# Row statistics written straight into lasting tiles, and an earlier combination in the inputs of the last attention

## What is computed

```python
x = L0(x)                              # window attention and an MLP, each behind a row norm
x = x + L1(group_norm(x))              # Fourier mixing
t = t + L2_attn(row_norm(t))           # landmark attention
t = t + L2_ffn(row_norm(t))            # two of eight experts for each token
t = t + L3_attn(row_norm(t))           # full attention, 12 heads of 16
t = t + L3_ffn(row_norm(t))            # one of eight experts for each token

def row_norm(v, eps):
    return (v - mean(v, -1)) / sqrt(var(v, -1) + eps)
```

## Time and profile before

| | |
|---|---|
| median of three runs | 1279.95 us (1279.7 to 1282.09) |
| the profiled execution | 1278.96 us, of it the span 1277.1 us |
| busy, share of the span | PE 82%, PEld 62%, DVE 46%, ACT 34%, POOL 22% |
| instructions | 21213; POOL 473 of those counted as busy |
| stage `l3p` and its last stores | about 902 to 987 us of the span |

### The profile page before, as it was taken

The page is one execution under the profiler, slowest core; times in us unless marked ns, Lnnn a source line. Parts: engine busy times, 40 slices in busy tenths (PEclk is TensorE's granted clock), DMA queues, the critical chain, the costliest instruction groups (busy, mean ns, idle before and its releaser), DMA issues. The chain is left out here.

```text
span 1277.1 us, 21213 instructions
## 1 busy us (share of the span) xinstructions
PE 1045.2 (82%) x7522; PEld 794.2 (62%) x7523; DVE 591.8 (46%) x1420; ACT 435.0 (34%) x880; POOL 286.9 (22%) x473
## 2 busy tenths in 40 slices
PE   6795999996998887999898379999376898767890
PEld 5594878874656665787897336666255455465670
DVE  4742655543114555455655634444364677331112
ACT  3653255553323222344440011111054466412330
POOL 5454301102001111000013042220563212103104
PEclk9865999998999998899787589999698999958895
DMA  7444843300112000100003621120244432044534
GB/s 89 120 115 126 188 92 86 93 7 1 38 62 72 16 0 0 50 2 1 1 2 100 180 56 50 49 49 31 59 107 102 129 97 72 3 142 113 148 112 105
DMA packets 118625, 91.41 MB, mean 72 GB/s; under 512 B 33010, under 2 KB 110924, under 8 KB 117900
## 3 DMA queue, kind: packets, MB, share of 16 engines
q1 hardware_dynamic: 106935, 76.31, 23.1%
q0 software_dynamic: 4992, 10.23, 3.7%
q10 hardware_dynamic: 6613, 3.74, 1.1%
HBM read 64.38 MB, written 28.12 MB: 72 GB/s over the span
## 5 line engine op out<-in xcount | busy, mean ns | idle before, releaser
L1227 DVE TENSOR_REDUCE l0a_nmax<-l0a_psS 98x2 f32<-98x392 f32 x96 | 54.2, 566 | 54.1 <-PE l0a_psS L1042 50.1
L871 DVE TENSOR_REDUCE l3a_nmax<-l3a_psS 128x2 f32<-128x512 f32 x96 | 62.0, 686 | 33.7 <-PE l3a_psS L725 33.4
L2428 POOL DMA_INDIRECT l2e_X<-xn,token_at x40 | 38.4, 961 | 128.2 <-PE l2e_psX L2443 74.9
L2493 ACT ACTIVATE l2e_H<-l2e_psH 128x512 f32<-128x512 f32 x40 | 21.7, 595 | 131.2 <-PE l2e_psH L2455 131.2
L827 ACT ACTIVATE l3a_PT<-l3a_psST 128x512 f32<-128x512 f32 x96 | 54.7, 596 | 29.0 <-PE l3a_psST L755 28.4
L2473 PEld LDWEIGHTS l2e_psY<-W2T,l2e_HT 128*128 128x128 f32 x320 | 51.4, 190 | 18.3 <-issue 18.2
L1177 ACT ACTIVATE l0a_PT<-l0a_psST 98x392 f32<-98x392 f32 x96 | 47.2, 497 | 42.2 <-PE l0a_psST L1084 41.9
L2473 PE MATMUL l2e_psY<-W2T,l2e_HT 128*128 x320 | 57.3, 332 | 3.4 <-DVE l2e_HT L2514 2.1
L2452 PE MATMUL l2e_psH<-W1T,l2e_XT 128*128 x80 | 40.9, 635 | 2.8 <-issue 2.0
L2520 DVE COPY l2e_Y<-l2e_psY 128x384 f32<-128x384 f32 x20 | 11.1, 557 | 65.1 <-PE l2e_psY L2473 65.1
L725 PE MATMUL l3a_psS<-l3a_KS,l3a_QS 96*128 96x256 bf16 x192 | 37.3, 275 | 3.9 <-DMA l3a_KS<-kd 2.9
(11 more groups left out here) (534 smaller groups left out, 2752.6 us busy)
## 6 DMA issues: line engine op xcount, KB each, us to landing
l3a_QS<-qd SPq DMA_DIRECT2D x72, 64.0 KB, 2.2
l3a_KS<-kd SPq DMA_DIRECT2D x72, 64.0 KB, 2.2
expert_W<-in_L_ffn_w SPq DMA_DIRECT2D x8, 576.0 KB, 4.7
rd<-l0q_r_p SPq DMA_DIRECT2D x24, 168.0 KB
ys<-l2e_Y SPq DMA_DIRECT2D x20, 192.0 KB, 1.9
l0a_QS<-qd SPq DMA_DIRECT2D x54, 64.0 KB
l0a_KS<-kd SPq DMA_DIRECT2D x54, 64.0 KB
W2T<-in_w2t SPq DMA_DIRECT2D x2, 1536.0 KB
```

Of the source, the lines that this page charges most:

```text
L871: nc.vector.tensor_reduce(nmax[k % 2][:, TI * u:TI * (u + 1), s], psS[item % 2][:, :].rearrange("p (t k) -> p t k", t=TI), AX.X, ALU.max, ...
L1227: mx = nc.vector.tensor_reduce(nmax[k % 2][0:WQ, 2 * j:2 * (j + 1), s], psS[item % 2][0:WQ, 0:2 * W0].rearrange("p (t k) -> p t k", t=2), ...
L2428: pool.indirect_dma_start(out=X[p % RING][:, t, :], out_offset=None, in_=G["xn"], in_offset=bass.IndirectOffsetOnAxis(ap=G["token_at"][:, ...
```

## The change

There are now two classes. `LoopStats` is the old one, used in the Fourier stage alone. The new `LnStats` has no tiles `mv` and `rstd`: `bn_aggr` writes mean and variance into a lasting tile `MV` (one pair per row tile), the add reads the variance there, and the power writes `RSTD` itself and raises `kept`. Its waits are plain ones. `MEAN` is now a view of `MV`, every second element. In `combined_inputs`, VectorE's `combine(i + 2)` stands ahead of the two remainders of image i.

```diff
--- before.py
+++ after.py
@@ -136,6 +136,40 @@
     def __init__(self, st, G, eps):
         self.nc, self.G, self.eps = st.nc, G, eps
         self.part = st.sb("stat_part", [P, 2, TI, 6])
+        self.ve = st.sb("stat_ve", [P, 2, TI])
+        self.exponent = st.sb("stat_exponent", [P, TI])
+        self.parts_done, self.mv_done, self.pow_done, self.kept = st.sems("stat_parts stat_mv stat_pow stat_kept")
+
+    def init(self, pool):
+
+        pool.sem_inc(self.kept, 2)
+        self.nc.gpsimd.memset(self.exponent[:, :], -0.5).then_inc(self.pow_done, 1)
+
+    def vector(self, nc, dve, i, u, *ready):
+
+        for sem, value in ready:
+            dve.wait_ge(sem, value)
+        dve.wait_ge(self.kept, i + 1)
+        for t in range(TI):
+            nc.vector.bn_stats(self.part[:, u, t, :], self.G["X"][:, TI * i + t, :]).then_inc(self.parts_done, 1)
+        dve.wait_ge(self.parts_done, TI * (i + 1))
+        for t in range(TI):
+            nc.vector.bn_aggr(self.G["MV"][:, TI * i + t, :], self.part[:, u, t, :]).then_inc(self.mv_done, 1)
+
+    def gpsimd(self, nc, pool, i, u):
+        pool.wait_ge(self.mv_done, TI * (i + 1))
+        nc.gpsimd.tensor_scalar(self.ve[:, u, :], self.G["MV"][:, TI * i:TI * (i + 1), 1], self.eps, None, ALU.add).then_inc(self.pow_done, 1)
+        pool.wait_ge(self.pow_done, i + 2)
+        nc.gpsimd.tensor_tensor(self.G["RSTD"][:, TI * i:TI * (i + 1)], self.ve[:, u, :], self.exponent[:, :], ALU.pow).then_inc(self.kept, 1)
+
+
+class LoopStats:
+
+
+
+    def __init__(self, st, G, eps):
+        self.nc, self.G, self.eps = st.nc, G, eps
+        self.part = st.sb("stat_part", [P, 2, TI, 6])
         self.mv = st.sb("stat_mv", [P, 2, TI, 2])
         self.ve = st.sb("stat_ve", [P, 2, TI])
         self.rstd = st.sb("stat_rstd", [P, 2, TI])
@@ -162,7 +196,7 @@
         pool.wait_ge(self.pow_done, 2 * i + 2)
         nc.gpsimd.tensor_tensor(self.rstd[:, u, :], self.ve[:, u, :], self.exponent[:, :], ALU.pow).then_inc(self.pow_done, 1)
         wait_all(pool, self.G["steady"], (self.pow_done, 2 * i + 3))
-        nc.gpsimd.tensor_copy(self.G["MEAN"][:, bass.ds(TI * i, TI)], self.mv[:, u, :, 0])
+        nc.gpsimd.tensor_copy(self.G["MV"][:, bass.ds(TI * i, TI), 0], self.mv[:, u, :, 0])
         nc.gpsimd.tensor_copy(self.G["RSTD"][:, bass.ds(TI * i, TI)], self.rstd[:, u, :]).then_inc(self.kept, 1)
 
 
@@ -1431,7 +1465,7 @@
         XC, SQ, XN, XS = two("XC", [P, TI, C]), two("SQ", [P, TI, C]), two("XN", [P, TI, C]), two("XS", [P, TI, C])
         FX, Z1, C1 = two("FX", [CH, 2, 3 * NF]), two("Z1", [CH, 2, 2 * NF]), two("C1", [CH, 2, 2 * NF])
         Z2, C2 = two("Z2", [SR, 2, 2, 2, CH]), two("C2", [SR, 2, 2, 2, CH])
-        stats = LnStats(st, G, 1e-5)
+        stats = LoopStats(st, G, 1e-5)
         psA = [st.ps(f"psA{u}") for u in range(2)]
         psB = [[st.ps(f"psB{u}{a}") for a in range(2)] for u in range(2)]
         w_in, zeroed, mean_mm, mean_done, xc_done, sq_done, var_mm, var_done, eps_done, std_done, rstd_done, xn_done, xs_done = st.sems(
@@ -2822,10 +2856,10 @@
                 u = i % 2
                 if i + 1 < B:
                     norm(i + 1)
+                if i + 2 < B:
+                    combine(i + 2)
                 qp.vector(nc, dve, QF[u][:, :, :], i, u)
                 kp.vector(nc, dve, KF[u][:, :, :], i, u)
-                if i + 2 < B:
-                    combine(i + 2)
                 qp.third(nc, dve, i, u)
                 kp.third(nc, dve, i, u)
             dve.wait_ge(pads_done, 2)
@@ -2930,9 +2964,10 @@
     def __init__(self, nc, w, consts, ctx):
         self.nc, self.w, self.consts, self.ctx = nc, w, consts, ctx
         self.G = {"consts": consts, "steady": ctx.enter_context(nc.semaphore("steady"))}
-        self.sb(ctx, X=(P, NT, C), MEAN=(P, NT), RSTD=(P, NT), ident=(P, P), early0=(P, EARLY), early1=(P, EARLY))
+        self.sb(ctx, X=(P, NT, C), MV=(P, NT, 2), RSTD=(P, NT), ident=(P, P), early0=(P, EARLY), early1=(P, EARLY))
         for name, n, dt in (("tri", P, BF16), ("onesb", P, BF16), ("earlier", NT * E + E, BF16), ("count", P, I32), ("token", NT, F16)):
             self.G[name] = ctx.enter_context(nc.sbuf_tensor(name, [P, n], dt))
+        self.G["MEAN"] = self.G["MV"][:, :, 0]
         self.dram(xw=(B * T, C), xr=(B * T, C), band=(NH, P * TW), xn=(B * T, C))
         self.dram(BF16, qd=(B, 3 * C * T), kd=(B, 3 * C * T))
```

## The result

The changed kernel takes 1263.9 us (median of 4 runs, 1260.85 to 1267.32) against 1279.83 for the kernel before on the same chip (4 runs, 1278.24 to 1282.09): ratio 0.9868, 95% interval [0.9833, 0.9903]. Ratios here are those on record with their intervals; the quotient of two medians (0.9876 here) can differ from them by 0.001. The forecast was 1265. The profiled execution of after took 1267.32 us, the longest of the four, so the two spans (1277.1 and 1265.5) differ by less than the medians do. I compare stage by stage.

A forecast was written before the change was run, and what follows sets the result against it. A chain of waits around several engines was taken to bound l3p, the inputs of the last attention. 12.0 + 0.9 + 0.8 + 1.0 = 14.7 us off 1278.96 gave 1264.3, so a median of 1265; range 1262 to 1271.

The forecast's parts named there:

- third normalising against the first: Inputs of the last attention (l3p): the third image's normalising starts at 929.7 in place of 933.11, 3.4 us earlier.
- the five steps to the last: Inputs of the last attention: steps from third to last normalising, 40.14 us before, become 8.6 us shorter in all.
- tails of l0a, l3a, l2o: Last statistics of window attention, full attention and landmark output end 0.9, 0.8 and 1.0 us earlier without copies.
- opening: Kernel start: first normalisings come 0.47 us earlier, but a load covers this, so nothing is gained.
- wider MV, address shift: The new tile is 64 bytes per partition wider and shifts later tiles; no row prices that, taken as 0.
- The mechanism in l3p: Inputs of the last attention: keys' remainder waits for ScalarE, the combination stands behind it; step 8.03 us, gain 12.0.
- VectorE's and ScalarE's loop: Inputs of the last attention: from normalising through remainders and key pieces to the next normalising, a step of about 6.1 us.
- GpSimd's loop: Inputs of the last attention: four gathers, add and power from reciprocal to reciprocal, step 6.4 to 6.9 us, 6.8 taken.
- Late gathers: Rival, inputs of the last attention: late gathers or held GpSimd, 1268 to 1271 us; chance 0.17, shared with clock 0.79.
- the three signs: Wrong if, in l3p, the combination waits on gathers, a gather takes clearly over 1.1 us, or granted clock is under 0.6.
- Only the copies count: Rival: the order does not matter; 0.47 us in each of seven images plus tails, 3.3 + 2.7, 1274 us; chance 0.07.
- A lower TensorE clock: Rival, inputs of the last attention: TensorE at 1.2 GHz becomes the bound, +7.8 us, 1288 us; chance 0.04.

The follow-up runs named there:

- e3: The changed kernel unaltered, run once more in a later session: 1265.55 us, ratio 0.9873 to the kernel before.
- e9: The changed kernel with the reciprocal written over the variance in MV and no RSTD tile, so later tiles are not shifted: 1259.89 us, ratio 0.982.
- e12: The kernel before with 64 unused bytes per partition behind the lists, ahead of the weights W1T and W2T: 1282.29 us, ratio 1.0013.
- e6: The kernel before with an unused tile of 64 bytes per partition behind MEAN, shifting all later tiles: 1285.34 us, ratio 1.0022.
- e11: The kernel before with 64 unused bytes per partition ahead of the list of experts per tile (tile_expert): 1284.87 us, ratio 1.0024.
- e2: The changed kernel with the old order, so the new statistics alone: the combination stands behind the remainders again; 1270.2 us, ratio 0.9911.
- e1: The kernel before with the new order alone: combination ahead of the two remainders, old statistics with their copies; 1274.93 us, ratio 0.9948.
- e5: The changed kernel with the combination between the two remainders, behind the queries' and ahead of the keys': 1266.73 us, ratio 0.9858.
- e4: The changed kernel with the addition of epsilon moved from GpSimd to VectorE: 1263.61 us, ratio 0.9844.

## Why the prediction was right, step by step

| term | predicted us | measured us |
|---|---|---|
| third normalising against the first | 3.4 | 3.99 (16.86 to 12.87) |
| the five steps to the last | 8.6 | 9.60 (40.14 to 30.54) |
| tails of l0a, l3a, l2o | 0.9, 0.8, 1.0 | 1.15, 1.14, 1.32 |
| opening | 0 | no more than 0.3, not in the sum |
| wider MV, address shift | 0 | -2.11 |
| sum | 14.7 | 15.1 |

The medians differ by 15.9 us (e3: 17.0). The mechanism is right, but the closeness of the sum is in part luck: every gain was put too low and the loss at nothing, and the two errors cancelled. All gains together measured 17.2 us, more than the 16.8 that the prediction called its upper bounds; without the loss the time would have come out at the low end of the range or under it, as e9 did (1259.89, against a kernel before of 1281.57). In those bounds 3.3 for the tails is a slip as well: three times 1.2 are 3.6.

- **The mechanism in l3p is right.** The wait of the keys' remainder, and the combination behind it, set the old step. With both parts of the change it is gone, and the last normalising comes 13.6 us earlier against the first (predicted 12.0, bounds 11.8 to 13.0).
- **The third normalising** came 3.99 earlier, not 3.4. In part this is TensorE's clock: the time from the first normalising to the third took 16.86, 16.49, 16.44 and 15.84 us in before, e12, e6 and e11, whose l3p is the same but for addresses, at a granted clock of 0.63, 0.66, 0.67 and 0.71 over its first 13 us. In after it took 12.87 at 0.67, so against e6, at the same clock, the gain is 3.57. The gains in l3p that are counted from before's 57.0 are high by some 0.4 for this reason.
- **VectorE's and ScalarE's loop was mis-sized:** 6.1 predicted, 5.70, 5.80 and 5.69 measured in the three steps that it sets. The failed statement is that the dropped waits on the steady semaphore are work of no time, "a gain from them over 0.03 us each is excluded by the 0.03 between gather and add". That bound was read from a gap on GpSimd. On VectorE they filled gaps of 0.20 and 0.13, and e2 shows 0.27 of gain per image. My sum was 6.16 before rounding, 0.46 more than the 5.70 measured; the rest of that is that an instruction starts up to 0.08 before the end that its predecessor's row gives (twice on this path: aggregate to remainder, third piece to normalising) and 0.03 in the remainder's length.
- **GpSimd's loop is right in sum, by errors that cancel:** 6.8 taken, 6.55 and 6.80 measured. Four gathers took 5.54 (944.62 to 950.16) where I had put 4.91; but the first one starts 0.19 after the reciprocal and not 0.43, and the statistics took 1.04 and not 1.57, because the third pieces had all but ended (950.30) when they began. In the next step the shares lie otherwise, 4.94 for the gathers and 1.39 for the statistics.
- **The tails** gained 0.25 to 0.34 more each than predicted (the landmark output's 1.32 lies over its bound of 1.2), for the same reason, as far as the rows show: the old waits stood on VectorE ahead of each aggregate and bn_stats. In window attention the first add of the tail starts 1.45 behind the last residual (304.01) where it started 1.65 behind it (304.83).
- **The wider tile** was priced at nothing, since no row priced it. It cost 2.11 us in l2e, and e6, e11 and e12 show that it is the address; e9, without the shift, has no such loss.
- **The opening:** the weight loads of TensorE's first transposes start at 14.85 in after against 15.13, 0.28 earlier, while the second normalising ends 1.52 earlier (7.76 against 9.28). The load and the warm-up behind it cover the rest, as predicted.
- **Rivals.** Late gathers: one wait of 0.66 in l3p, not five. Longer gathers did come (1.16 to 1.22 in many, 0.95 alone). So two of the three signs that the prediction named for being wrong did show, a wait on a gather and gathers of over 1.1; their price was small, since the longest step was still the 6.80 that was taken for GpSimd. The Trainium skill's rule ("SBUF — State Buffer", section "Who interferes with whom"), that a VectorE instruction with two SBUF inputs contends with a GpSimd instruction that reads SBUF, agrees in direction: the add took 0.56 beside the remainders (936.00) and 0.24 alone, the power 1.02 and 0.73. A GpSimd step of 7.8 did not come in after. "Only the copies count" falls with e1: the order alone wins 8.8 us in l3p. A lower TensorE clock falls with the stretches at 1.00 from the third normalising on.

## What to carry to other kernels

Before moving an instruction, look for the engine that is next after the one relieved: the order alone ran into GpSimd, and only with its copies gone did the step reach VectorE's length, in three of five steps. When code loses waits, read the gap that they leave on each engine, not on one of them. And a tile that grows moves all tiles behind it: keep the layout the same (here by writing the reciprocal over the variance) or time an unused pad of that size by itself, before the gain or loss is put down to the edit. Compare stages at the same granted clock: with the same instructions one stretch of l3p took 15.84 to 16.86 us and the Fourier stage 115.6 to 119.3.

## What the runs showed of the hardware that was not expected

- 64 bytes of shift, with nothing in the instructions changed but addresses, lengthen one stage from 137.3 to 139.6 us (e6, e11, e12); without a shift in the new kernel it takes 136.3 (e9).
- The extra waits ahead of bn_stats and of the aggregate cost VectorE 0.17 and 0.10 us per image (0.20 and 0.13 before, 0.03 after), though all that they waited for was VectorE's own instruction just before, by the profile.
- A gather's issue on GpSimd takes 0.95 us when VectorE lets it be, and up to 1.76 beside VectorE's two-input work (e5). Work taken off GpSimd (e4) came back as longer gathers.
